# Expert results: from gated products on GpSimd, a scratch tensor and a closing pass, to products on VectorE and accumulating stores into the output rows

## The chip, the core and the metric

The kernel runs on one core of a Trainium2 chip. A core has TensorE (PE, matrix products into PSUM; PEld is its weight load), VectorE (DVE), ScalarE (ACT), GpSimd (POOL) and SyncE (SP, which here only issues transfers), each with an instruction queue of its own, and 16 DMA engines that move data between DRAM and SBUF. The engines wait for each other by semaphores. The metric is the device time of one launch in microseconds; the median of several runs is compared.

## The reference

A token mixer (two selective state-space scans, forward and backward) followed by a mixture of experts, for 2 batches of 2048 tokens of width 256. The part that the change touches is the end of it:

```
x = x + ga * mixer(...)
h = layernorm(x) * (1 + cb) + sb
# 8 experts, each token goes to its best 2, with weights from a softmax
for e in range(8):
    a  = silu(xs @ w1[e].T + b1[e])
    x2 = a @ w2[e].T + b2[e]
    x3 = xs @ w3[e].T + b3[e]
    y += sum over the token's two places of x2 * x3 * (expert of the place == e)
z = shared expert of h
x = x + gb * (y + z)        # gb: one row of 256 per batch
```

`xs` is the token's row times its routing weight. 4096 tokens with two experts each make 8192 (token, expert) pairs.

## The kernel before

The program is written by hand: each engine has a straight list of instructions, and the order of work is that list and the semaphore waits in it. There are three stages.

**Scan stage.** 16 steps of 16 units. It is not touched, but for a few constants that GpSimd makes in the last step (`constants`) for the stages behind.

**Router and shared expert.** A loop over 8 blocks of 512 tokens. SyncE loads a block (`load_block`), VectorE normalises and ranks the experts, TensorE and the others compute the shared expert, whose gated result VectorE adds to the block in `x1` (`add_shared`, semaphore `s_x1`). ScalarE scales the token's row by its weight into `send` (`scale_tokens`), adds the number of the pair as column 257, and GpSimd scatters the rows (`scatter`, an indirect transfer of 128 rows) to the region of the row's expert in `slot_scratch`. Places behind an expert's last row are filled with rows of zeros whose number points to spare rows ("trash"): ScalarE zeroes `send`, SyncE stores it twice (L676) early in the stage, ScalarE's first `scale_tokens` waits for both stores (`trash_kept`), and after all scatters SyncE copies one such row block behind each expert (L703).

**Expert stage.** 72 tiles of 128 rows (8192 pairs and up to one part-filled tile for each expert; spare tiles at the end). `tile_loop` writes out tiles 0 to 7, a hardware loop of 7 rounds of 8 tiles, and tiles 64 to 71. In tile s TensorE does the product with w1 and w3 of tile s (`hidden`, L1906), turns the silu of tile s-1 (L1916) and the input of tile s+1 (L1897), and does the product with w2 of tile s-2 (`result`, L1926). VectorE adds the biases: to the 512 columns of tile s (`bias_hidden`, L1555, into `hx`, ring of 4), copies the row numbers out (L1557, `target_u`), and to the 256 columns of tile s-2 (`bias_result`, L1564, into `yt`, ring of 4). Each of the two begins with a `value_load`: the engine's sequencer reads the tile's expert number from SBUF into a register and checks it, since the bias row is addressed by it. ScalarE copies and does silu. GpSimd multiplies x2 by x3 (L894) and stores the 128 rows by an indirect transfer (L898) to the row of their pair in `yout_scratch`. SyncE loads the input of tile s+4 (L696) when its buffer is free.

When all stores have landed comes a closing pass over 8 blocks: SyncE loads both results of each token from `yout_scratch` (L723), VectorE adds the two (L1583), multiplies by gb (L1585), adds to `x1` (L1587), and SyncE stores the block to the output (L692).

In the rows below the tiles' names are those of the tensor that the memory was first given to: `h` stands for the small tiles of the expert stage (xt, hx, hs, yt), `w` for the experts' weights and, in the closing pass, the loaded results.

## Time and profile before

| | |
|---|---|
| median of 3 runs | 2269.19 us (2267.29 to 2276.48) |
| the profiled execution | 2270.67 us |
| its span, first to last instruction | 2268.9 us |
| TensorE clock granted, mean | 0.853 |
| busy share | PE 80%, DVE 88%, ACT 61%, POOL 80% |

The span begins with the first instruction and ends with the last; the 1.8 us that the time has more lie around it. The shares are means over stages with different limits: DVE and POOL are busy nine tenths in the scan stage (up to about 1780 us), PE in the router stage and the expert stage (to about 2224 us), and neither in the closing pass.

### The profile page before, as it was taken

What the parts mean: (1) busy time and instruction counts of PE and PEld (TensorE: products, weight loads), DVE (VectorE), ACT (ScalarE), POOL (GpSimd) and SP (SyncE); (2) the same over time, 40 slices, a digit from 0 to 9 for tenths busy, and PEclk for the clock granted to TensorE, in tenths of its full rate; (3) what the DMA queues carried; (4) which work ended last, traced back from release to release, by engine and by line L of the source; (5) the groups of instructions that cost most, each with busy time, mean ns of one, the idle gap of its engine ahead of it and who ended that gap; (6) DMA issues with size and microseconds to landing.
All of it is one profiled execution on the core that took longest, in us unless ns stands there. A gap on an engine that the chain in (4) does not pass through costs nothing.

```text
span 2268.9 us, 23450 instructions
## 1 busy us (share of the span) xinstructions
PE 1821.4 (80%) x6088; PEld 754.4 (33%) x6089; DVE 2006.8 (88%) x2219; ACT 1374.9 (61%) x2348; POOL 1823.1 (80%) x718
## 2 busy tenths in 40 slices
PE   7687787978786978778797878797855799999991
PEld 3222232313231323223232323232321366656561
DVE  7899999999999999999999999999999876633335
ACT  4667768585867676776858576767755333323330
POOL 3499999999999999999999999999999443435551
PEclk9787888879787879788797979797967799999996
DMA  7734434343534344343434353444434541222226
GB/s 285 221 85 107 120 100 124 95 112 100 121 105 99 107 118 113 105 112 95 124 102 109 102 118 104 105 112 109 97 95 137 173 171 56 77 78 86 86 86 238
DMA packets 135965, 266.05 MB, mean 117 GB/s; under 512 B 20225, under 2 KB 39937, under 8 KB 134705
## 3 DMA queue, kind: packets, MB, share of 16 engines
q1 hardware_dynamic: 126448, 236.97, 38.9%
q0 software_dynamic: 6528, 17.87, 2.2%
q10 hardware_dynamic: 2880, 9.96, 1.1%
q8 instruction: 45, 0.74, 0.1%
q14 instruction: 64, 0.52, 0.1%
HBM read 198.62 MB, written 67.15 MB: 117 GB/s over the span
## 4 chain that ended last, share of the span: by engine, by line
DVE 43%; PE 25%; issue 14%; ACT 8%; POOL 6%; DMA 3%; SPq 1%; DVEq 0%; ACTq 0%; POOLq 0%
DVE hst L1315 28%; DVE dbu L1301 9%; PE psum L1906 6%; PE psum L1843 4%; POOL hst L800 4%; PE psum L1926 3%; ACT psum L1064 3%; PE psum L1718 2%; PE psum L1855 2%; PE psum L1652 2%; PE psum L1645 2%; PE psum L1676 1%; DMA b_rep<-bc_scratch 1%; ACT L1064 1%; PE psum L1706 1%
## 5 line engine op out<-in xcount | busy, mean ns | idle before, releaser
L800 POOL TENSOR_TENSOR hst<-hst,c_rep 128x2048 f32<-128x2048 f32 x255 | 1150.5, 4527 | 51.2 <-DVE hst L1315 31.8
L1064 ACT ACTIVATE psum<-dt_rep,neg_a 128x512 f32<-128x512 f32 x1024 | 687.9, 683 | 400.6 <-DVE hst L1315 398.7
L1315 DVE TENSOR_TENSOR_SCAN hst<-psum,state,dbu 128x512 f32<-128x512 f32 x768 | 920.8, 1254 | 0.0
L1301 DVE TENSOR_TENSOR dbu<-psum,b_rep 128x2048 f32<-128x2048 f32 x192 | 434.0, 2260 | 12.6 <-PE psum L1706 7.1
L1706 PE MATMUL psum<-dt,same 32*128 32x512 f32 x384 | 251.7, 739 | 171.7 <-DVE dbu L1301 166.9
L1718 PE MATMUL psum<-hst,same 128*32 128x512 f32 x2048 | 323.0, 788 | 79.3 <-POOL hst L800 71.0
L788 POOL TENSOR_TENSOR dbu<-dtu_rep,b_rep 128x2048 f32<-128x2048 f32 x64 | 291.4, 4553 | 25.8 <-DVE hst L1315 25.7
L1315 DVE TENSOR_TENSOR_SCAN hst<-psum,dbu 128x512 f32<-128x512 f32 x256 | 291.6, 1196 | 1.8 <-ACT psum L1064 1.7
L1664 PE MATMUL psum<-xp,taps 128*128 128x512 f32 x512 | 240.6, 614 | 2.1 <-DVE sp_tmp L1294 0.9
L1718 PEld LDWEIGHTS psum<-hst,same 128*32 128x32 f32 x2048 | 73.7, 139 | 340.5 <-issue 216.3
L1706 PEld LDWEIGHTS psum<-dt,same 32*128 32x128 f32 x384 | 64.4, 207 | 328.4 <-DVE dbu L1301 232.9
L1652 PE MATMUL psum<-xnT,w_in 128*128 128x512 f32 x256 | 139.8, 672 | 41.6 <-ACT sz L996 41.6
L1645 PE MATMUL psum<-xnT,w_in 128*128 128x512 f32 x256 | 132.8, 645 | 18.4 <-ACT xc L1008 17.4
L878 POOL DMA_INDIRECT slot_scratch<-send,slot_u x64 | 64.5, 1008 | 98.8 <-ACT send L1161 64.9
L1906 PE MATMUL psum<-w,h 128*128 x288 | 139.8, 608 | 1.9 <-ACT h L1182 1.9
L1664 PEld LDWEIGHTS psum<-xp,taps 128*128 128x128 f32 x512 | 96.7, 194 | 133.1 <-issue 130.8
L1555 DVE TENSOR_TENSOR h<-psum,b 128x512 f32<-128x512 f32 x72 | 49.8, 691 | 99.4 <-PE psum L1906 99.4
L1714 PE MATMUL psum<-xc,diag_d 128*128 128x512 f32 x128 | 97.3, 852 | 32.6 <-DVE sz L1286 32.5
L1676 PE MATMUL psum<-w_out,sz 128*128 128x256 f32 x512 | 119.2, 387 | 4.0 <-DVE sz L1286 4.0
L898 POOL DMA_INDIRECT yout_scratch<-h,target_u x72 | 72.5, 1008 | 59.4 <-POOL h L894 56.5
L1843 PE MATMUL psum<-h2T,sw 128*128 128x512 f32 x256 | 115.4, 605 | 1.4 <-ACT g_silu L1148 1.4
L1194 ACT ACTIVATE h<-psum 128x256 f32<-128x256 f32 x72 | 27.6, 383 | 143.7 <-PE psum L1916 143.7
(166 smaller groups left out, 2293.7 us busy)
## 6 DMA issues: line engine op xcount, KB each, us to landing
dt_rep<-dt_scratch SPq DMA_DIRECT2D x256, 256.0 KB, 4.5
taps<-taps_scratch SPq DMA_DIRECT2D x64, 256.0 KB, 3.0
b_rep<-bc_scratch SPq DMA_DIRECT2D x64, 256.0 KB, 5.1
c_rep<-bc_scratch SPq DMA_DIRECT2D x64, 256.0 KB, 7.9
dt_scratch<-dt SPq DMA_DIRECT2D x64, 256.0 KB, 2.0
dtu_rep<-dtu_scratch SPq DMA_DIRECT2D x256, 64.0 KB, 1.9
h<-slot_scratch SPq DMA_DIRECT2D x72, 128.5 KB, 2.1
sp_tmp<-t_scratch SPq DMA_DIRECT2D x16, 512.0 KB, 4.8
```

The costliest lines, as they stand in the source:

```text
L788: nc.gpsimd.tensor_tensor(dbu[:, U % DBU, :, :], dtu_rep[:].broadcast_to((P, NG, TB)), b_rep[U // UNITS % 2][:], ALU.mult).then_inc(pool_m ...
L800: nc.gpsimd.tensor_tensor(h, h, c_rep[q % 2][:], ALU.mult).then_inc(prod_done, 1)
L1064: nc.scalar.activation(psum[:, PS_A + i, :], dt_rep[:, G % 2, j, :], ACT.Exp, scale=neg_a[:, q % 2, u, i:i + 1]).then_inc(exp_done, 1)
L1301: nc.vector.tensor_tensor(dbu[:, U % DBU, :, :], psum[:, PS_U:PS_U + 1, :].broadcast_to((P, NG, TB)), b_rep[U // UNITS % 2][:], ALU.mult). ...
L1315: nc.vector.tensor_tensor_scan(time_order(hst[:, U % RING, i, :], backward), time_order(psum[:, PS_A + i, :], backward), time_order(dbu[:, ...
L1645: ins = nc.tensor.matmul(psum[:, bank, :], w_in[:, q % 2, k, c * P:(c + 1) * P], xnT[:, q % 2, k, :], start=(k == 0), stop=(k == KD - 1))
L1652: ins = nc.tensor.matmul(psum[:, bank, :], w_in[:, q % 2, k, DI + c * P:DI + (c + 1) * P], xnT[:, q % 2, k, :], start=(k == 0), stop=(k == ...
L1664: ins = nc.tensor.matmul(psum[:, bank, :], taps[:, c % 2, j, :], xp[:, c % 2, at:at + TB], start=(j == 0), stop=(j == TAPS - 1))
L1706: nc.tensor.matmul(psum[:, PS_U, :], same[part, :], dtu[part, c, :], start=True, stop=True).then_inc(u_full, 1)
L1718: ins = nc.tensor.matmul(psum[CH * j:CH * (j + 1), PS_Y, :], same[:, 0:CH], hst[:, (GN * G + j) % RING, i, :], start=False, stop=(i == NG ...
L1843: ins = nc.tensor.matmul(psum[:, bank, :], w[:, k, c * P:(c + 1) * P], h2T[:, j % 2, k, :], start=(k == 0), stop=(k == KD - 1))
L1906: ins = nc.tensor.matmul(psum[:, 2 + r % 2, :], xtT[:, r % 2, k * P:(k + 1) * P], w13[:, bass.ds(e * KD + k, 1), :].rearrange("p a n -> p ...
```

## The change

GpSimd no longer multiplies. VectorE does x2 times x3 (`bias_result`), and before it x3 times gb (`gate_rows`), for which it needs, row by row, gb of the row's batch: ScalarE makes half of it (`begin_gate`, gb of batch 0 times the row's first flag) and VectorE the rest; the two flags are two new columns of the scattered rows. The output tensor gets one row for each token; `x1` is stored to it block by block while the router loop runs (`store_block`), and GpSimd's indirect store of a tile adds its 128 rows to the output rows in DRAM (`compute_op=ALU.add`). Two experts can hold the same token, so a tile's store must not be in flight with one of the expert before: it waits for the stores of tiles s-2 and s-3 always, and for that of tile s-1 only where the expert changes; the count to wait for is looked up in a table (`follows_u`) by a `value_load`. The closing pass and `yout_scratch` are gone. The spare rows behind the output are set to zero by one more store.

```diff
 @@ router stage, SyncE
+            sp.dma_start(out[TOKENS:OUT_ROWS].rearrange("(a p) d -> p a d", p=P), trash[:, :, 0:DM]
+                         ).then_inc(trash_kept, 16)
...
+            def store_block(p):
+                n = TAKEN[p]
+                sp.wait_ge(s_x1, 2 * p + 2)
+                sp.dma_start(out[n * TB:(n + 1) * TB].rearrange("(p t) d -> p t d", t=NT), x1[:, rows_of(n), :]
+                             ).then_inc(f_out, 16)
             for p in range(4, NBLK):
                 load_block(p)
+                store_block(p - 4)
+            store_block(NBLK - 4)
...
 @@ expert stage, SyncE
             def tiles(s, r):
                 if not (isinstance(s, int) and s + 4 >= TILES):
                     sp.wait_ge(target_kept, s + 1)
+                    sp.wait_ge(gate_done, s + 1)
                     wait_apart(sp)
                     load_tile(s + 4, r)
...
-            for i in range(NBLK):
-                for k in range(2):
...
-                    sp.dma_start(yg[:, r, :].rearrange("p (t d) -> p t d", t=NT),
-                                 yout_dram[first:first + TB, :].rearrange("(t p) d -> p t d", p=P)
-                                 ).then_inc(y_back[r], 16)
-                if i >= 3:
-                    store_block(i - 3)
...
 @@ expert stage, GpSimd
             def tiles(s, r):
-                pool.wait_ge(y_biased, s + 1)
-                nc.gpsimd.tensor_tensor(yt[:, r % 4, :], yt[:, r % 4, :], hx[:, r % 4, DM:2 * DM], ALU.mult
-                                        ).then_inc(y_done, 1)
                 pool.wait_ge(y_done, s + 1)
+                for back in (3, 2):
+                    if not (isinstance(s, int) and s < back):
+                        pool.wait_ge(y_stored[(r - back) % 4], landed_by(s, r, back))
+                if isinstance(s, int) and s < 5:
+                    if s > 0:
+                        pool.wait_ge(y_stored[(r - 1) % 4], landed_by(s, r, 1))
+                else:
+                    count = nc.gpsimd.value_load(follows_u[0:1, bass.ds(s, 1)], min_val=16, max_val=4 * TILES)
+                    pool.wait_ge(y_stored[(r - 1) % 4], count)
                 wait_apart(pool)
                 nc.gpsimd.indirect_dma_start(
-                    yout_dram, bass.IndirectOffsetOnAxis(ap=target_u[:, r:r + 1], axis=0), yt[:, r % 4, :], None
-                    ).then_inc(y_stored[r % 4], 16)
+                    out, bass.IndirectOffsetOnAxis(ap=target_u[:, r:r + 1], axis=0), yt[:, r % 4, :], None,
+                    compute_op=ALU.add).then_inc(y_stored[r % 4], 16)
...
 @@ ScalarE
                 if m == 0:
-                    act.wait_ge(trash_kept, 32)
+                    act.wait_ge(trash_kept, 48)
...
+                nc.scalar.activation(send[:, m % 4, :, DM + 1:ROW],
+                                     batch_flag[:, n // SEG:n // SEG + 1, :].broadcast_to((P, NT, BATCH)), ACT.Copy
+                                     ).then_inc(scaled, 1)
...
+            def begin_gate(s, r, m):
+                act.wait_ge(xt_loaded[r % 4], m * 16 + 16)
+                if not (isinstance(s, int) and s < 2):
+                    act.wait_ge(gated, s - 1)
+                nc.scalar.activation(row_gate[:, r % 2, :], fmod[:, 0, 3, :], ACT.Copy, scale=xt[:, r % 4, DM + 1:DM + 2]
+                                     ).then_inc(gate_begun, 1)
...
 @@ expert stage, VectorE
+            def gate_rows(s, r):
+                dve.wait_ge(gate_begun, s + 1)
+                nc.vector.scalar_tensor_tensor(row_gate[:, r % 2, :], fmod[:, 1, 3, :], xt[:, r % 4, DM + 2:DM + 3],
+                                               row_gate[:, r % 2, :], ALU.mult, ALU.add).then_inc(gate_done, 1)
+                dve.wait_ge(gate_done, s + 1)
+                dve.wait_ge(hx_done, s + 1)
+                nc.vector.tensor_tensor(hx[:, r % 4, DM:2 * DM], hx[:, r % 4, DM:2 * DM], row_gate[:, r % 2, :], ALU.mult
+                                        ).then_inc(gated, 1)
...
                 nc.vector.tensor_tensor(yt[:, r % 4:r % 4 + 1, :], psum[:, 6 + r % 2:7 + r % 2, 0:DM],
                                         b2[:, bass.ds(e, 1), :], ALU.add).then_inc(y_biased, 1)
+                dve.wait_ge(y_biased, s + 1)
+                dve.wait_ge(gated, s + 1)
+                nc.vector.tensor_tensor(yt[:, r % 4, :], yt[:, r % 4, :], hx[:, r % 4, DM:2 * DM], ALU.mult
+                                        ).then_inc(y_done, 1)
 
             def tiles(s, r):
                 bias_hidden(s, r)
                 if not (isinstance(s, int) and s < 2):
                     bias_result(s - 2, (r - 2) % UNROLL)
+                gate_rows(s, r)
...
-            def finish(i):
...
-            for i in range(NBLK):
-                finish(i)
```

GpSimd's constants change by some small instructions, two small table instructions are added on VectorE behind the router loop, and the scattered rows are 259 numbers long, not 257.

On VectorE one tile of the hardware loop, the list before (ISA rows are register arithmetic of the sequencer; L1555 is `bias_hidden`, L1564 `bias_result`):

```order
L1551 TENSOR_LOAD expert_u
L1551 ISA x2
L1555 ISA [waits y_done,hx_full]
L1555 TENSOR_TENSOR h<-psum,b 128x512
L1557 CAST target_u<-h 128x1
L1560 TENSOR_LOAD expert_u
L1560 ISA x2
L1564 ISA [waits y_stored1,y_full]
L1564 TENSOR_TENSOR h<-psum,tin 128x256
```

And the same tile of the changed list (L1602 is `bias_hidden`, L1620 and L1624 are `bias_result`, L1608 and L1612 are `gate_rows`):

```order
L1602 TENSOR_TENSOR h<-psum,b 128x512
L1604 CAST target_u<-h 128x1
L1616 TENSOR_LOAD expert_u
L1616 ISA x2
L1620 ISA [waits y_stored1,y_full]
L1620 TENSOR_TENSOR h<-psum,tin 128x256
L1624 TENSOR_TENSOR h<-h 128x256 [waits gated,y_biased]
L1608 SCALAR_TENSOR_TENSOR h<-fmod,h 128x256 [waits gate_begun]
L1612 TENSOR_TENSOR h<-h 128x256 [waits hx_done,gate_done]
```

Three engine instructions came behind L1620, of which L1624 and L1612 wait for the instruction just before them; the TENSOR_LOAD of the next tile's `bias_hidden` now stands behind L1612, the last of them.

On GpSimd one tile of the hardware loop, before:

```order
L893 REGISTER_ALU
L894 TENSOR_TENSOR h<-h 128x256 [waits y_biased]
L898 DMA yout_scratch<-h,target_u 10240x256 [waits y_done]
L893 REGISTER_ALU
L894 TENSOR_TENSOR h<-h 128x256 [waits y_biased]
```

And in the changed list (L927 is the accumulating store, to the output):

```order
L916 REGISTER_ALU
L924 ISA [waits y_stored2,y_stored1,y_done]
L924 TENSOR_LOAD follows_u
L924 ISA x2
L927 DMA out_x<-h,target_u 6144x256 [waits y_stored3]
```

The product is gone from GpSimd; in its place stand a wait for two earlier stores, a register load, and a wait for the store just before.

## Rows read from the trace of the kernel before

**Rows 1.** Stretches: length, busy PE, PEld, DVE, ACT, POOL (count), clock, DMA share, GB/s
```profile
1950.00:2000.00 50.00, 46.51 (x163) 28.20 (x162) 21.49 (x56) 15.79 (x34) 15.71 (x16) 0.99 0.24 72
...
2170.40:2194.90 24.50, 24.50 (x97) 14.62 (x96) 9.41 (x24) 8.30 (x24) 13.77 (x17) 1.00 0.28 86
...
2220.60:2268.90 48.30, 2.59 (x11) 1.56 (x10) 30.04 (x27) 0.59 (x2) 5.56 (x7) 0.58 0.78 271
```

**Rows 2.** TensorE's branch at the end of the hardware loop's rounds
```profile
L491 PEldq COMPARE_BRANCH  x7: 83/227/247, 2047.8 to 2194.9; - x7
```

**Rows 3.** Timeline: the last hidden tile
```profile
2219.67 0.69 DVE L1555 TENSOR_TENSOR h<-psum,b 128x512 f32<-128x512 f32 x1 [1.32 <-PE psum L1906]
```

**Rows 4.** The chain that ended last, closing pass: start, us, what
```profile
2264.64 1.22 DVE x L1587
```

**Rows 5.** Groups by line in the expert stage
```profile
L898 POOL DMA_INDIRECT yout_scratch<-h,target_u x72 | 72.5, 1008 | 59.4 <-POOL h L894 56.5 <-issue 3.0
L894 POOL TENSOR_TENSOR h<-h 128x256 f32<-128x256 f32 x72 | 51.5, 715 | 64.8 <-DVE h L1564 64.6
```

**Rows 6.** Timeline, one tile of the hardware loop
```profile
2103.57 0.69 DVE L1555 TENSOR_TENSOR h<-psum,b 128x512 f32<-128x512 f32 x1 [1.22 <-PE psum L1906]
...
2104.87 0.42 DVE L1564 TENSOR_TENSOR h<-psum,tin 128x256 f32<-128x256 f32 x1 [0.55 <-PE psum L1926]
```

**Rows 7.** VectorE's sequencer (DVEq), 2103.5 to 2106.7: min/median/max ns, first and last start
```profile
L1563 DVEq EVENT_SEMAPHORE  x1: 21/21/21, 2104.3 to 2104.3; - x1
L1551 DVEq TENSOR_LOAD <-expert_u x1: 303/303/303, 2105.0 to 2105.0; - x1
L1554 DVEq EVENT_SEMAPHORE  x1: 21/21/21, 2105.7 to 2105.7; - x1
L1555 DVEq FUSED_REGOPS  x2: 57/57/57, 2103.5 to 2106.5; - x2
```

**Rows 8.** Timeline: three kinds of VectorE instruction on 256 columns
```profile
1797.08 1.66 DVE L1345 SCALAR_TENSOR_TENSOR h<-x,fmv,fmod 128x256 f32<-128x256 f32 x4
...
1801.35 0.43 DVE L1384 TENSOR_TENSOR cmp_eq<-score 128x256 f32<-128x256 f32 x1
1801.81 0.42 DVE L1385 TENSOR_TENSOR cmp_eq<-cmp_eq,lower 128x256 f32<-128x256 f32 x1
```

**Rows 9.** One line's own durations (ns)
```profile
L1345 DVE SCALAR_TENSOR_TENSOR h<-x,fmv,fmod x32: 474/478/480, 1786.8 to 1943.5; 128x256 f32<-128x256 f32 x32
```

**Rows 10.** VectorE and GpSimd at the same time (timeline)
```profile
1777.62 3.27 DVE L1482 TENSOR_TENSOR hst<-hst,c_rep 128x2048 f32<-128x2048 f32 x1
...
1769.77 8.97 POOL L800 TENSOR_TENSOR hst<-hst,c_rep 128x2048 f32<-128x2048 f32 x2
...
1816.86 0.43 DVE L1384 TENSOR_TENSOR cmp_eq<-score 128x256 f32<-128x256 f32 x1
...
1816.46 1.27 POOL L878 DMA_INDIRECT slot_scratch<-send,slot_u  x1 [0.20 <-issue]
```

**Rows 11.** Transfers of the expert stage: KB each, median us to landing
```profile
h<-slot_scratch SPq DMA_DIRECT2D x72, 128.5 KB, 2.1
...
yout_scratch<-h,target_u POOLq DMA_INDIRECT x72, 2.5
slot_scratch<-trash_scratch SPq DMA_DIRECT2D x3, 128.5 KB, 2.6
```

**Rows 12.** SyncE: eight transfers, each behind a value_load
```profile
1983.20 9.53 SPq L703 DMA_DIRECT2D slot_scratch<-trash_scratch  x8
```

**Rows 13.** Early router stage: transfers, and the timeline behind the trash stores
```profile
slot_scratch<-send SPq DMA_DIRECT2D x1, 1028.0 KB, 13.7
...
1784.63 0.58 SPq L676 DMA_DIRECT2D slot_scratch<-send  x1
...
1806.26 1.69 ACT L1159 ACTIVATE send<-h,weight 128x256 f32<-128x256 f32 x4
...
1810.02 1.22 PE L1843 MATMUL psum<-h2T,sw 128*128 128x512 f32 x1 [1.41 <-ACT g_silu L1148]
```

More of the change, by code:

```diff
@@ L429, in mixer_and_experts @@
         target_kept = sem("target_kept")
-        y_back = [sem(f"y_back{r}") for r in range(8)]
-        f_fin = sem("f_fin")
+        gate_begun = sem("gate_begun")
+        gate_done = sem("gate_done")
+        gated = sem("gated")
         f_out = sem("f_out")
@@ L2002 @@
            for name, v in arrays.items()}
[L2003 removed]
+    out = nc.dram_tensor("out_x", (OUT_ROWS, DM), F32, kind="ExternalOutput").ap()
     mixer_and_experts(nc, aps, out)
```

81 lines of the change are left out of this document (44 added, 37 removed).

## Prediction, made before the change was run

> **What bounds the kernel now.** I read the profile from its end. The stretch behind the last tiles ([rows 1], third row) is 48.3 us long and holds 2.6 us of TensorE work: this is the closing pass. The timeline of the last tiles and the chain of waits give its place: VectorE adds the bias to the last hidden tile at 2219.67 [rows 3], its last instruction of the closing pass starts at 2264.64 [rows 4], and the span ends at 2268.9. From that bias addition, which I call H, to the end are 49.2 us.
>
> Before it, in the expert stage, TensorE is busy all of the time at full clock, 24.50 of 24.50 us in one round of 8 tiles, VectorE 9.4 us [rows 1], its second row. The branch at a round's end comes seven times from 2047.8 to 2194.9 [rows 2], so a tile takes 147.1 / 48 = 3.065 us. TensorE sets this pace, and whatever the change puts on other engines is free only while their own time for a tile stays below 3.065 us.
>
> The shares hide one thing: VectorE's 9.4 us of 24.5 counts instructions, not its sequencer. Between an instruction and one behind a `value_load`, the sequencer reads and checks the register. After the bias addition at 2104.87 [rows 6] it reaches the wait behind the load only at 2105.7, and the next instruction's own register step and start take 0.1 more (2106.5 to 2106.6) [rows 7]: 0.8 + 0.06 + 0.1, about 0.95 to 1.0 us. The other load begins at 2103.57 [rows 6] and its wait is reached at 2104.3 [rows 7]; with the register step the earliest start of L1564 is 0.95 us behind that of L1555. Today both stand in time that VectorE would idle anyway.
>
> **The closing pass goes.** What takes its place is the way of the last results to DRAM. After H VectorE adds the bias of tile 69 (0.9 us on), multiplies (0.46 more to its start, 0.42 long): the product of 69 is ready at H + 1.8. Behind that come the gate of tile 71 (to its last issue 2.2 us on) and the last two bias additions, each behind a load of 0.8 us and each followed by its product: bias of 70 at H + 3.0, its product 0.5 on, bias of 71 at H + 4.3 to 4.4, its product ready at H + 5.3. For one store GpSimd then needs a register load (not in this trace on GpSimd; on SyncE eight transfers with one each take 9.53 us in all [rows 12], so a pitch of 1.29 with some 0.5 of transfer instruction, which leaves 0.8), the 0.8 us that the indirect store now starts behind its releaser (59.4 / 72 [rows 5]), and the landing, 2.5 us behind the start for the plain store [rows 11].
>
> The trace has no accumulating store. From below: a copy DRAM to DRAM of 128 rows lands in 2.6 us and a read of as many in 2.1 us [rows 11], so an added read can be nearly free: 2.5 us. From above: a read and a write in series, 2.1 + 2.5 = 4.6 us, unless the adding itself is slow, which no row excludes. I take 3.5 us, the middle. One store is then 0.8 + 0.8 + 3.5 = 5.1 us from its releaser to its landing. Tile 69 lands at H + 6.9, tile 71 waits for it and lands at H + 12.0, and the end comes some 0.4 us later. Saved: 49.2 - 12.4 = **36.8 us**.
>
> **What GpSimd's waits cost in the loop.** The chain through GpSimd is "the store two tiles back has landed, then 5.1 us": 2.55 us for a tile, less than TensorE's 3.065. At an expert's first tile it is 5.1 us for one tile, some 2 us late, eight times at most. Queued behind is the next store alone, and who waits for stores is VectorE's `bias_result` of four tiles on, 12 us later. So I cost these waits at nothing; the cover is the ring of four, and it goes if the landing takes more than about 5 us (below).
>
> **VectorE gets the products.** Per tile: a scalar_tensor_tensor (0.478 us [rows 9]) and two tensor_tensor of 256 columns (0.42 us each [rows 8]). By busy time VectorE has 9.41 / 8 = 1.18 us a tile and would have 2.50: fits under 3.065. By its list it does not. From the start of L1602: 0.95 to the bias addition L1620; 0.46 to the product L1624, since an instruction that waits for its predecessor starts 0.46 behind it (1801.35 to 1801.81 [rows 8]), and 0.03 for its second wait; 0.34 to L1608, which waits for nothing late (independent ones overlap by 0.085: four of 0.478 in 1.66 us [rows 8, 9]); 0.48 + 0.04 to L1612, which waits for L1608, and 0.03 for its second wait; then the load of the next tile, 0.95 to 1.0, which now begins only when L1612 has been issued. Sum: 0.95 + 0.49 + 0.34 + 0.55 + 1.0 = **3.33 us**. VectorE's sequencer becomes the bound of the loop, though VectorE's busy share stays at three quarters.
>
> In the tiles written out the loads need no address arithmetic and the sum is about 3.10. Against before: 56 tiles x (3.33 - 3.065) = 14.8, seven branches of VectorE's own at 0.15 = 1.0, 15 tiles x 0.06 = 0.9: **+16.7 us**. The five terms are each good to some 0.03 to 0.05 us, so the tile may come to 3.2 as well as to 3.45.
>
> [...] VectorE's record here is 0.303 us [rows 7]. [...]
>
> **ScalarE** gets one instruction of 256 columns, and has 8.30 of 24.5 us busy [rows 1]: free, and its result is asked for one tile later. **SyncE's** loads wait for L1608 of tile s, some 2 us later than now, with three tiles (9 us) in hand and 2.1 us to landing: free. PE's clock: a stretch with TensorE 93% busy had 0.99 ([rows 1], its first row), and at 3.33 us a tile it is 92% busy, so I leave it at full.
>
> **The router stage.** Eight stores of 512 KB of `x1` lie in a stage in which the DMA engines are a quarter busy; SyncE's waits for `s_x1` come before those for the later loads anyway: nothing. The zeroing of the spare rows is another matter. Both trash stores (2.1 MB) are issued by 1784.63 and the second lands 13.7 us later, at 1798.3 [rows 13]. 2.1 MB more behind them at the same 230 to 280 GB/s lands at 1805.8 to 1807.4. ScalarE's first scaling, at 1806.26, waits for it, and TensorE stands 1.41 us for ScalarE at 1810.02 [rows 13]: so this instruction is on the path. I take +0.6 us, and +0.2 for the flag column's instruction, here and before the last scatter. GpSimd's constants are some short instructions in gaps of the scan stage: nothing.
>
> **Sum**, against the profiled execution: 2270.67 - 36.8 + 16.7 + 0.8 = 2251.4 us. The profiled execution lies 1.5 us over the median, so **2250 us** is what I forecast for the median.
>
> **The rivals.**
> *VectorE keeps up* (chance 0.16). If the sequencer runs further ahead than I read, the loop stays at 3.065: 2250 - 16.7 = 2233 us. For it: the busy time of 2.50 us. Against: in rows 6 and 7 the load always starts behind the instruction before it.
> *The accumulating store is slow* (0.13), the one that ends on the other side. Two landings back means (1.6 + L) / 2 us a tile, with L from start to landing; at L = 5.1 that is my 3.33. The gain is gone at L = 5.4: 71 x ((1.6 + 5.4) / 2 - 3.06) + 2 x 1.9 = 35 us. At L = 6 it is 3.8 us a tile, 2233 + 52.5 + 5 = 2291 us. For it: no row shows the adding. Against: the 4.6 us of a read and a write in series.
> *GpSimd and VectorE hold each other up* (0.04). VectorE's product of 2048 columns with two SBUF inputs took 3.27 us, to 1780.89, beside GpSimd's products, which ended at 1778.74; the 2.15 us from there are just what 2048 columns take at 0.42 us for 256 with the start taken off, so it had waited [rows 10]. If GpSimd's indirect store held VectorE so, each tile would wait 0.3 to 1.0 us, and the time would be about 2250 + 72 x 0.5 = 2286 us. Against: beside L878 the product L1384 took its 0.43 us, and it was GpSimd that took 1.27 [rows 10]. [...]
>
> **How the numbers follow.** The likeliest, VectorE's list as the bound, has 0.64, with a range of its own of 2243 to 2259; the last 0.03 are for what I don't see. 0.5% of 2269 is 11.3 us, about what a measurement of this kernel can tell from no change. Faster by more (under 2257.8): the first rival's 0.16, some 0.53 of the likeliest, 0.01 of the slow store: 0.70. Within: the likeliest's upper tail, a tile of 3.45 us or a landing of 5 us: 0.18. Slower (over 2280.5): most of the slow store and of the contention: 0.12. The range of 2232 to 2268 leaves out the slow cases and takes in the first rival.
>
> **What the profile will show.** In a round of the hardware loop of 26 to 27.5 us instead of 24.5: TensorE under 95% busy, with waits for ScalarE's silu and, through it, for VectorE's L1602; L1602 no longer waiting for L1906. Starts of L1612 and the next L1602 0.95 to 1.0 us apart. The accumulating store landing 3 to 4 us behind its start, GpSimd idle for stores only at experts' first tiles. The end 12 us behind the last L1602. The first L1188 at 1806.5 to 1808. Wrong it goes first if the landing is over 5 us, if TensorE's clock falls at 92% busy, or if rounds are 24.5 us as before.

## The result, and the profile after

| | before | after |
|---|---|---|
| median of 5 runs, us | 2269.86 (2267.29 to 2276.48) | 2255.35 (2247.88 to 2256.75) |
| profiled execution, us (its span) | 2270.67 (2268.9) | 2256.75 (2255.0) |

The ratio on record is 0.9924, 95% interval 0.9911 to 0.9938: faster by 0.76%. (It is not the ratio of the two medians, which differ by 14.5 us, 0.64%.) 19 us were forecast.

The stretches that answer to [rows 1]: the router's last part, one round of 8 tiles and somewhat less, and the last tiles with the end.
```profile
1950.00:2000.00 50.00, 47.51 (x173) 29.54 (x171) 23.00 (x60) 15.80 (x37) 15.94 (x16) 1.00 0.26 87
2180.00:2204.60 24.60, 24.12 (x88) 13.33 (x88) 17.89 (x47) 11.13 (x30) 11.61 (x8) 1.00 0.50 80
2220.60:2255.00 34.40, 23.43 (x90) 13.50 (x89) 20.32 (x50) 10.19 (x28) 15.74 (x11) 0.94 0.45 62
```
The end with almost no TensorE work is gone, and VectorE does twice the work in a stretch of the loop (17.89 us in 24.6, where it was 9.41 in 24.5). TensorE reads as busy at 98%, and yet it completes 88 matmuls in 24.6 us where it completed 97 in 24.5: the ends of matmuls are modelled, so its busy time hides that it is being kept waiting. The granted clock stayed at 1.00 in the loop. What tells the pace is the branch at a round's end, which answers to [rows 2]:
```profile
L499 PEldq COMPARE_BRANCH  x7: 83/227/246, 2053.5 to 2215.4; - x7
```
161.9 us for 48 tiles are 3.373 us a tile (3.065 before). The groups by line of the expert stage say who waits. VectorE's hidden bias before:
```profile
L1555 DVE TENSOR_TENSOR h<-psum,b 128x512 f32<-128x512 f32 x72 | 49.8, 691 | 99.4 <-PE psum L1906 99.4
```
and the lines of after:
```profile
L927 POOL DMA_INDIRECT out_x<-h,target_u x72 | 113.0, 1569 | 155.2 <-DMA out_x<-h,target_u 70.3 <-issue 47.0 <-DVE h L1624 37.9
L1602 DVE TENSOR_TENSOR h<-psum,b 128x512 f32<-128x512 f32 x72 | 49.8, 692 | 53.1 <-issue 39.7 <-PE psum L1950 13.4
L1620 DVE TENSOR_TENSOR h<-psum,tin 128x256 f32<-128x256 f32 x72 | 30.6, 425 | 14.7 <-issue 8.8 <-PE psum L1970 1.3 <-DMA out_x<-h,target_u 0.6
```
VectorE's hidden bias waited for TensorE before (99.4 us in all); now 39.7 of its 53.1 us are "issue", time in which nothing that the profile shows was awaited. VectorE's result bias waits 0.6 us in all for landed stores. Of the 70.3 us that the profile puts to landings ahead of GpSimd's stores, 31 are no wait. The profile names the semaphore that came last, and at this pace a store often lands just when the next one starts (a landing takes 3.7 us or more, and from the store at 2172.74 to the next at 2176.45 are 3.71). In the trace GpSimd lags its data by up to 8.6 us at the first tiles and has caught up by tile 24; from there to tile 67 a store starts 1.4 to 1.8 us behind the end of its product whether or not a landing is named, and 2.2 to 3.1 us behind it at five tiles, where it waits for the store before. One tile of VectorE's timeline, to be laid beside [rows 6]:
```profile
2101.49 0.69 DVE L1602 TENSOR_TENSOR h<-psum,b 128x512 f32<-128x512 f32 x1 [0.59 <-issue]
2102.10 0.14 DVE L1604 CAST target_u<-h 128x1 uint32<-128x1 f32 x1
2102.36 0.42 DVE L1620 TENSOR_TENSOR h<-psum,tin 128x256 f32<-128x256 f32 x1
2102.81 0.42 DVE L1624 TENSOR_TENSOR h<-h 128x256 f32<-128x256 f32 x1
2103.16 0.48 DVE L1608 SCALAR_TENSOR_TENSOR h<-fmod,h 128x256 f32<-128x256 f32 x1
2103.67 0.42 DVE L1612 TENSOR_TENSOR h<-h 128x256 f32<-128x256 f32 x1
2104.93 0.69 DVE L1602 TENSOR_TENSOR h<-psum,b 128x512 f32<-128x512 f32 x1 [0.84 <-issue]
```
From L1602 to L1620, L1624, L1608, L1612 and the next L1602 the starts are 0.87, 0.45, 0.35, 0.51 and 1.26 us apart (the last one 0.98 at the tile behind it). The sequencer's rows for its two register reads show why the last one varies (ns, shortest/median/longest):
```profile
L1598 DVEq TENSOR_LOAD <-expert_u x72: 300/311/632, 1999.2 to 2240.6; - x72
...
L1616 DVEq TENSOR_LOAD <-expert_u x72: 297/303/676, 2011.5 to 2245.4; - x72
```
Most reads take 0.30 us; 15 of the 144 take over 0.45, the longest 0.68. `expert_u` is the table of the tiles' expert numbers, which the kernel keeps in SBUF. The other two parts of this `value_load` are register arithmetic, 0.19 us in the median, and the check of the value, 0.02 us:
```profile
L1598 DVEq FUSED_REGOPS  x121: 53/190/211, 1999.8 to 2241.1; - x121
...
L1598 DVEq SEQ_ASSERT  x72: 23/23/35, 2000.0 to 2241.3; - x72
```

The end, on the timeline, answers to [rows 3, 4]: the last hidden bias, which the prediction calls H, and the last four stores (tiles 68 to 71).
```profile
2241.53 0.69 DVE L1602 TENSOR_TENSOR h<-psum,b 128x512 f32<-128x512 f32 x1 [0.48 <-issue]
...
2242.88 1.55 POOL L927 DMA_INDIRECT out_x<-h,target_u  x1 [2.94 <-DMA out_x<-h,target_u]
...
2245.03 1.55 POOL L927 DMA_INDIRECT out_x<-h,target_u  x1 [0.60 <-issue]
...
2248.08 1.55 POOL L927 DMA_INDIRECT out_x<-h,target_u  x1 [1.49 <-DVE h L1624]
2250.02 1.57 POOL L927 DMA_INDIRECT out_x<-h,target_u  x1 [0.39 <-issue]
```
From H to the end are 13.5 us (49.2 before). The chain of waits has the stores' way to DRAM (start, us):
```profile
2238.38 3.70 DMA out_x<-h,target_u
2242.88 3.76 DMA out_x<-h,target_u
```
To cut the execution into stages, I take the first and the last start of the hidden bias, of before and after:
```profile
L1555 DVE TENSOR_TENSOR h<-psum,b x72: 690/691/693, 2002.5 to 2219.7; 128x512 f32<-128x512 f32 x72
```
```profile
L1602 DVE TENSOR_TENSOR h<-psum,b x72: 691/692/693, 2005.6 to 2241.5; 128x512 f32<-128x512 f32 x72
```
and the last links of the scan in the chain of waits, of before and after:
```profile
1770.45 7.08 DVE hst L1315 x6
```
```profile
1772.60 7.08 DVE hst L1358 x6
```

| stage | before | after | difference | forecast |
|---|---|---|---|---|
| to the scan's last links | 1770.5 | 1772.6 | +2.1 | 0 |
| router, to the first hidden bias | 232.1 | 233.0 | +0.9 | +0.8 |
| first to last hidden bias | 217.1 | 235.9 | +18.8 | +16.7 |
| H to the end | 49.2 | 13.5 | -35.7 | -36.8 |

The sum, -13.9, is the difference of the two profiled executions. Of the signs that the prediction named, most came: 27.0 us for a round of 8 tiles, landings of 3.7 to 4.4 us in the chain of waits, 13.5 us behind the last L1602. TensorE under 95% busy did not: it reads as 98%.

### The profile page after: what moved, and what is told of

The parts are those of the page before. It is cut to its first block, busy times and chain, and to the rows that moved or that the text cites. A ratio compares the mean times of both kernels' runs of the same rounds, so it can differ in the third digit from the quotient of the medians.

```text
span 2255.0 us, 24227 instructions
## 1 busy us (share of the span) xinstructions
PE 1829.4 (81%) x6088; PEld 756.1 (34%) x6089; DVE 2068.6 (92%) x2413; ACT 1409.9 (63%) x2436; POOL 1811.8 (80%) x652
## 3 DMA queue, kind: packets, MB, share of 16 engines
q0 software_dynamic: 13440, 17.93, 4.8%
## 4 chain that ended last, share of the span: by engine, by line
DVE 49%; PE 16%; issue 16%; ACT 10%; DMA 4%; DVEq 3%; POOL 2%; SPq 1%; POOLq 0%; ACTq 0%
DVE hst L1358 31%; DVE dbu L1344 10%; PE psum L1887 4%; ACT psum L1093 3%; PE psum L1696 3%; PE psum L1899 2%; PE psum L1762 2%; DMA out_x<-h,target_u 2%; ACT L1093 1%; PE psum L1750 1%; POOL hst L807 1%; DVEq L1598 1%; DVE h L1608 1%; DVE sz L1329 1%; DVE h L1620 1%
## 5 line engine op out<-in xcount | busy, mean ns | idle before, releaser
L1344 DVE TENSOR_TENSOR dbu<-psum,b_rep 128x2048 f32<-128x2048 f32 x192 | 436.3, 2273 | 15.7 <-PE psum L1750 9.9
L1750 PE MATMUL psum<-dt,same 32*128 32x512 f32 x384 | 257.5, 755 | 158.1 <-DVE dbu L1344 153.3
L1762 PE MATMUL psum<-hst,same 128*32 128x512 f32 x2048 | 306.1, 752 | 86.6 <-POOL hst L807 78.0
L927 POOL DMA_INDIRECT out_x<-h,target_u x72 | 113.0, 1569 | 155.2 <-DMA out_x<-h,target_u 70.3
L1696 PE MATMUL psum<-xnT,w_in 128*128 128x512 f32 x256 | 150.4, 718 | 48.4 <-ACT sz L1025 48.4
L1689 PE MATMUL psum<-xnT,w_in 128*128 128x512 f32 x256 | 132.1, 642 | 18.4 <-ACT xc L1037 17.4
L1738 PE MATMUL psum<-sp_tmp,w_dt 16*128 16x512 f32 x128 | 94.1, 843 | 43.1 <-ACT sp_tmp L1064 42.4
L1720 PEld LDWEIGHTS psum<-w_out,sz 128*128 128x128 f32 x512 | 97.0, 192 | 35.7 <-issue 18.1
L1758 PE MATMUL psum<-xc,diag_d 128*128 128x512 f32 x128 | 88.2, 777 | 21.1 <-DVE sz L1329 20.3
```

The source lines that it names most:

```text
L1344: nc.vector.tensor_tensor(dbu[:, U % DBU, :, :], psum[:, PS_U:PS_U + 1, :].broadcast_to((P, NG, TB)), b_rep[U // UNITS % 2][:], ALU.mult). ...
L1696: ins = nc.tensor.matmul(psum[:, bank, :], w_in[:, q % 2, k, DI + c * P:DI + (c + 1) * P], xnT[:, q % 2, k, :], start=(k == 0), stop=(k == ...
L1720: ins = nc.tensor.matmul(psum[:, bank, half * DM:(half + 1) * DM], sz[:, c, tok], w_out[:, q % 2, c, :], start=(c == 0), stop=(c == NC - 1))
L1750: nc.tensor.matmul(psum[:, PS_U, :], same[part, :], dtu[part, c, :], start=True, stop=True).then_inc(u_full, 1)
L1762: ins = nc.tensor.matmul(psum[CH * j:CH * (j + 1), PS_Y, :], same[:, 0:CH], hst[:, (GN * G + j) % RING, i, :], start=False, stop=(i == NG ...
```

## The experiments

The theory: VectorE's sequencer sets the pace of the loop, by register reads in series with waits. The rivals: GpSimd's accumulating store sets it, or VectorE's executing time, or the three products contend with the stores. Each kernel below is the changed kernel with the edit shown, or with several where it says so. "A tile" is the branch's first to last time over 48.

**One read more.**
```diff
             def bias_result(s, r):
+                nc.vector.value_load(expert_u[0:1, bass.ds(s, 1)], min_val=0, max_val=NE - 1)
                 e = nc.vector.value_load(expert_u[0:1, bass.ds(s, 1)], min_val=0, max_val=NE - 1)
```


> VectorE reads the expert number once more for each tile, right ahead of the read for the result's bias; nothing else changes. If VectorE's sequencer sets the pace of the loop (my theory), each tile gets longer by what the added read takes there: 0.30 us for the record of the load, about 0.2 us of register arithmetic and 0.02 us of range check, 0.5 to 0.55 us in all, so a tile goes from 3.37 to some 3.9 us and the time from 2255 to 2255 + 72 x 0.53 = 2293 us. If VectorE's executing time or TensorE sets the pace (the rival that VectorE keeps up, or a loop that is slower for GpSimd's store), an added read is hidden and the time stays at 2255.


Measured: 2294.1 us (ratio to before 1.0108, 1.0080 to 1.0136), 3.960 us a tile:
```profile
L499 PEldq COMPARE_BRANCH  x7: 83/227/251, 2056.6 to 2246.7; - x7
```
0.59 us more for each tile (0.5 to 0.55 expected), none of it hidden. VectorE's busy time for a tile did not rise; its list did.

**The number kept in a register.**
```diff
             def bias_hidden(s, r):
                 e = nc.vector.value_load(expert_u[0:1, bass.ds(s, 1)], min_val=0, max_val=NE - 1)
+                numbers[r] = e
...
-            def bias_result(s, r):
-                e = nc.vector.value_load(expert_u[0:1, bass.ds(s, 1)], min_val=0, max_val=NE - 1)
+            def bias_result(s, r, kept=True):
+                e = numbers[r] if kept else nc.vector.value_load(expert_u[0:1, bass.ds(s, 1)], min_val=0, max_val=NE - 1)
...
-                    bias_result(s - 2, (r - 2) % UNROLL)
+                    bias_result(s - 2, (r - 2) % UNROLL, r > 1)
```


> VectorE keeps the expert number read for the hidden bias in a register and uses it again for the result's bias two tiles later, so 54 of the 72 second reads go (in each run of 8 tiles the first two results still read theirs). If the sequencer sets the pace, the bias addition L1620 starts 0.70 to 0.75 us behind L1602 and not 0.87 to 0.95, since L1602 itself takes 0.69: 0.15 to 0.2 us less in 6 of 8 tiles, a tile of 3.23 to 3.26 us and 2255 - 9 = 2246 us (2243 to 2249). If something else sets the pace (GpSimd's store or TensorE), no change: 2255.


Measured: 2246.3 us (0.9898, 0.9879 to 0.9918), 3.258 us a tile, as expected. (56 of the 72 second reads are gone, not 54.)

**Another order, both reads kept.**
```diff
                 bias_hidden(s, r)
+                fill_gate(s, r)
                 if not (isinstance(s, int) and s < 2):
                     bias_result(s - 2, (r - 2) % UNROLL)
                 gate_rows(s, r)
+                if not (isinstance(s, int) and s < 2):
+                    gate_result(s - 2, (r - 2) % UNROLL)
```
`fill_gate` has the scalar_tensor_tensor L1608 that stood in `gate_rows`, and `gate_result` the product L1624 that stood in `bias_result`, each with its waits.


> The same instructions of VectorE in another order, both reads kept: hidden bias, gate of the rows (scalar_tensor_tensor), result's bias, product with the gate, product of the result. No instruction waits any more for the one right ahead of it. By my list: 0.71 to the gate, 0.90 behind the read to the result's bias, 0.40 and 0.40 to the two products, 0.95 behind the next read: 3.36 us a tile against 3.37, so no change, 2252 to 2256 us, since the reads still follow each other with 0.8 us of sequencer each. If what costs is the waits for VectorE's own results (0.49 and 0.55 in my sum, the rival reading), the two shorter pitches give 0.2 us a tile and the time is 2241.


Measured: 2244.7 us (0.9881, 0.9860 to 0.9902), and the tile fell to 3.075 us: TensorE's pace. My list was wrong. The rival reading was right in kind, and gave 0.2 us a tile where 0.30 went; the median stayed above its 2241. The timeline, and the sequencer's read of the result's number (L1618) in the same tile:
```profile
2103.53 0.69 DVE L1602 TENSOR_TENSOR h<-psum,b 128x512 f32<-128x512 f32 x1 [0.65 <-PE psum L1958]
2104.14 0.14 DVE L1604 CAST target_u<-h 128x1 uint32<-128x1 f32 x1
2104.20 0.47 DVE L1608 SCALAR_TENSOR_TENSOR h<-fmod,h 128x256 f32<-128x256 f32 x1
2104.94 0.42 DVE L1622 TENSOR_TENSOR h<-psum,tin 128x256 f32<-128x256 f32 x1 [0.26 <-PE psum L1978]
2105.28 0.41 DVE L1614 TENSOR_TENSOR h<-h 128x256 f32<-128x256 f32 x1
2105.61 0.42 DVE L1628 TENSOR_TENSOR h<-h 128x256 f32<-128x256 f32 x1
```
```profile
L1618 DVEq TENSOR_LOAD <-expert_u x1: 600/600/600, 2103.6 to 2103.6; - x1
```
The read starts at 2103.6, ahead of the cast (2104.14) and of the gate (2104.20), which stand before it in the program. So the sequencer hands instructions on and reads ahead, while they wait their turn. Even a read of 0.60 us is hidden. In the changed kernel each of L1624 and L1612 waits for the instruction right ahead of it, and that wait holds the sequencer: the next read starts only behind the start of L1612.
```profile
L1598 DVEq TENSOR_LOAD <-expert_u x1: 582/582/582, 2103.8 to 2103.8; - x1
```
That is the read at the tile above: L1612 started at 2103.67, the read at 2103.8 (0.10 us behind it in the median of all tiles). Other work lies between producer and consumer in the new order: L1614 and L1628 start 0.34 and 0.33 us behind the instruction ahead, where L1624 and L1612 of the changed kernel start 0.45 and 0.51 us behind the one they wait for.

**No read at all.** The order and the waits of the changed kernel; the biases are those of expert 0 for every tile, so the other experts' biases are left out.
```diff
-                e = nc.vector.value_load(expert_u[0:1, bass.ds(s, 1)], min_val=0, max_val=NE - 1)
+                e = 0
```


> VectorE reads no expert number: both bias additions take the rows of expert 0 for every tile (a change of the computation: biases of the other experts are left out), so both register reads, their checks and the address arithmetic go, and the order and all waits of the changed kernel stay. If the two reads are what makes the list long, the sum is 0.71 + 0.49 + 0.34 + 0.55 + 0.62 = 2.7 us a tile, TensorE sets the pace again at 3.07 and the time is 2236 to 2241. If waits for VectorE's own results or the store are enough by themselves, the tile stays at 3.3 and the time at 2252 or more.


Measured: 2240.7 us (0.9873, 0.9855 to 0.9892), 3.067 us a tile. So neither the reads nor the waits make the loop slow by themselves: it takes both, in series. The accumulating store and all three products are still there, so neither the store nor VectorE's executing time is the bound.

**Both edits.** The kept number and the other order.


> The kept number and the other order together. By the list of VectorE's sequencer: 0.71 + 0.40 + 0.40 + 0.40 + 0.95 = 2.86 us where the number is kept, which is under TensorE's 3.065, and about 3.3 in the two tiles of 8 with a second read: a mean of 3.10 to 3.13, so 2255 - 72 x 0.25 = 2237 us (2233 to 2242). If GpSimd's accumulating store is what makes the loop slower than before, there is no gain here: 2255.


Measured: 2236.6 us (0.9852, 0.9832 to 0.9873), 3.067 us a tile:
```profile
L499 PEldq COMPARE_BRANCH  x7: 83/227/246, 2044.4 to 2191.6; - x7
```
The time is the expected one, the tile is shorter than the 3.10 to 3.13 of my list. In the loop the other order alone does as much. The two profiled executions are 15.7 us apart all the same: 13.2 of it lie ahead of the tiles, and behind the last hidden bias the other order took 17.3 us and this kernel 14.5, since GpSimd's stores ran later there. How much of the 8 us between the medians is the edit's is not shown. What remained in the trace was one late stretch near the start, where VectorE's bias waits for a place in the ring of four:
```profile
2040.46 0.42 DVE L1625 TENSOR_TENSOR h<-psum,tin 128x256 f32<-128x256 f32 x1 [2.81 <-DMA out_x<-h,target_u]
```
It comes from GpSimd's first stores, which the program always lets wait for the one before (at tiles 1 to 4 the table's count is 0 where the expert does not change, and the kernel's register load is set to take 16 or more):
```profile
2015.12 1.55 POOL L927 DMA_INDIRECT out_x<-h,target_u  x1 [3.10 <-DMA out_x<-h,target_u]
2020.13 1.55 POOL L927 DMA_INDIRECT out_x<-h,target_u  x1 [3.46 <-DVE h L1631]
2024.81 1.65 POOL L927 DMA_INDIRECT out_x<-h,target_u  x1 [3.13 <-DMA out_x<-h,target_u]
```

**A free start**, on top of both edits.
```diff
+            for r in range(4):
+                nc.gpsimd.dma_start(dtu_dram[0, r:r + 1], dtu_dram[1, r:r + 1]).then_inc(y_stored[r], 16)
+            for r in range(4):
+                pool.wait_ge(y_stored[r], 16)
...
-                if isinstance(s, int) and s < 5:
-                    if s > 0:
-                        pool.wait_ge(y_stored[(r - 1) % 4], landed_by(s, r, 1))
-                else:
+                if not (isinstance(s, int) and s == 0):
```
(and every count on `y_stored` 16 higher).


> The kept number and the other order, and besides that the first stores no longer always wait for the one before: the four landing semaphores begin at 16 (a tiny copy for each, waited for ahead of the tiles), so that the register's value can be used from the second tile on. In the run with both edits the first five stores start 4.7 us apart, GpSimd is 6 us behind its tiles by then, and VectorE's bias additions at tiles 11 to 15 come 3 us late in sum because the ring of four is full. If that reading is right, those 3 us go: 2236.5 - 3 = 2233.5 us (2231 to 2235). If the late tiles have another cause, 2236.5.


Measured: 2236.3 us (0.9840, 0.9815 to 0.9865). The hidden biases of both edits and of this kernel:
```profile
L1605 DVE TENSOR_TENSOR h<-psum,b x72: 690/692/693, 1996.6 to 2216.4; 128x512 f32<-128x512 f32 x72
```
```profile
L1606 DVE TENSOR_TENSOR h<-psum,b x72: 690/692/693, 2003.0 to 2220.3; 128x512 f32<-128x512 f32 x72
```
From first to last: 219.8 and 217.3 us, so the late stretch is gone from the trace (before had 217.1). But the profiled execution reached its tiles 6.4 us later; the scan's last links started 6.5 us later, in a stage that both have alike. The two were timed once more, side by side:


> The kernel with both edits once more, timed beside the next two: 2236 us, between 2233 and 2239.

> The kernel with the free start once more, beside the one above. The late tiles 11 to 15 went in the trace of its first run (217.3 us from the first to the last hidden bias against 219.8), so it should be 2.5 us faster than the one above: ratio 0.9989. If front stages differ by more than that between runs, the difference is not told apart.


Measured: 2236.4 us (0.9853, 0.9835 to 0.9871) and 2241.2 us (0.9859, 0.9836 to 0.9883), with 219.2 and 217.4 us between the hidden biases. The 2 us are real in the trace and not to be told in the time, since runs of the second spread over 14 us (2230.8 to 2245.1).

**No wait at the spare tiles**, on top of the free start.
```diff
+            counted(nc.vector.tensor_scalar(expert[:], expert[:], float(NE - 1), None, ALU.min))
+            settle()
             counted(nc.vector.tensor_tensor(changes[:, 1:TILES], expert[:, 1:TILES], expert[:, 0:TILES - 1],
                                             ALU.not_equal))
```


> The free start, and the mark of an expert's first tile is worked out after the numbers are cut to the last expert, so the first spare tile no longer waits for the last real tile. In the trace of the free start that store starts 4.44 us behind the one before it, at 2222.41, and could start at 2220.8; with the two-back waits behind it the last landing comes 1.5 to 1.8 us earlier. One more short instruction of VectorE ahead of the tiles costs 0.2. So 1.5 us faster than the free start, 2232 to 2234 us; if the last stores are set by their data and not by this wait, no difference.


Measured: 2237.4 us (0.9853, 0.9831 to 0.9875). In its trace the last hidden bias is at 2222.0 and the span ends at 2235.6: 13.6 us, where the free start had 14.3 in both its traces (2220.3 to 2234.6 in the first). 0.7 us and not 1.5 to 1.8, and not to be told in the time.

**The product back on GpSimd**, ahead of its store, everything else as changed.
```diff
             def tiles(s, r):
+                pool.wait_ge(y_biased, s + 1)
+                pool.wait_ge(gated, s + 1)
+                nc.gpsimd.tensor_tensor(yt[:, r % 4, :], yt[:, r % 4, :], hx[:, r % 4, DM:2 * DM], ALU.mult
+                                        ).then_inc(y_done, 1)
                 pool.wait_ge(y_done, s + 1)
...
-                dve.wait_ge(y_biased, s + 1)
-                dve.wait_ge(gated, s + 1)
-                nc.vector.tensor_tensor(yt[:, r % 4, :], yt[:, r % 4, :], hx[:, r % 4, DM:2 * DM], ALU.mult
-                                        ).then_inc(y_done, 1)
```


> The product of the result with the gated x3 goes back to GpSimd, ahead of its accumulating store; the rest is as in the changed kernel. VectorE's list then is 0.9 + 0.34 + 0.55 + 1.0 = 2.8 us a tile, under TensorE's 3.065. GpSimd's own list is 0.72 for the product, some 0.9 for the wait for it, the register load and the check, 1.57 for the store's descriptors and 0.1 to 0.3 to the next start: 3.3 to 3.5 us a tile. My theory: GpSimd takes VectorE's place as the bound, 3.4 us a tile, 2250 to 2262 us, no gain from undoing this part. The rival: VectorE's list was the only thing too long and GpSimd has room, 3.07 us a tile and 2235.


Measured: 2308.9 us (1.0180, 1.0152 to 1.0208), slower than before, 193.7 / 48 = 4.035 us a tile. GpSimd is the bound, as I said, but by far more than the 3.4 us that I said. The gate's product on VectorE, the product on GpSimd, GpSimd's store, and one store with the product behind it:
```profile
L1616 DVE TENSOR_TENSOR h<-h x72: 424/832/1387, 2002.8 to 2285.0; 128x256 f32<-128x256 f32 x72
```
```profile
L918 POOL TENSOR_TENSOR h<-h x72: 741/1315/1567, 2009.6 to 2297.5; 128x256 f32<-128x256 f32 x72
```
```profile
L931 POOL DMA_INDIRECT out_x<-h,target_u x72 | 115.4, 1603 | 121.0 <-DMA out_x<-h,target_u 95.3 <-DVE h L1616 17.0 <-issue 8.8
```
```profile
2123.36 1.73 POOL L931 DMA_INDIRECT out_x<-h,target_u  x1 [1.63 <-DMA out_x<-h,target_u]
2124.54 1.32 POOL L918 TENSOR_TENSOR h<-h 128x256 f32<-128x256 f32 x1
```
GpSimd's product takes 1.3 and not 0.715 us [rows 5], but VectorE is not the cause: the product in the last line runs from 2124.54 to 2125.86, and VectorE has no instruction between 2124.09 and 2126.00. The product's record begins some 0.55 us before that of the store ahead of it ends, and ends some 0.76 us behind it (0.75 to 0.77 at nearly all tiles), so it stands in line behind GpSimd's own store; at three tiles only, beside a VectorE product of 1.36 to 1.39 us, it took 1.57. From store to store are then 1.60 for the store, 0.76 for the product and 121.0 / 72 = 1.68 us before the next store, 4.04 in all. I had 1.57, 0.72 and 1.0 to 1.2: the term that I had too small is the time between the product and the store, with the wait for the product and the register load in it. VectorE's product is held up: it took 0.83 us or more at the 46 tiles where GpSimd's product ran beside it, and its 0.42 us at the other 26. Since VectorE waited for GpSimd in this kernel (98.3 of the 106.8 us that it stood idle ahead of the hidden biases are put to L918), this is not what set its pace. In the changed kernel, where GpSimd has the indirect store alone, VectorE's two-input products keep their 0.425 us:
```profile
L1624 DVE TENSOR_TENSOR h<-h x72: 424/425/491, 2013.2 to 2246.7; 128x256 f32<-128x256 f32 x72
...
L1612 DVE TENSOR_TENSOR h<-h x72: 424/424/429, 2006.8 to 2244.1; 128x256 f32<-128x256 f32 x72
```

**A plain store.** The results overwrite the output rows and are not added to them, so the output is not the sum.
```diff
-                    out, bass.IndirectOffsetOnAxis(ap=target_u[:, r:r + 1], axis=0), yt[:, r % 4, :], None,
-                    compute_op=ALU.add).then_inc(y_stored[r % 4], 16)
+                    out, bass.IndirectOffsetOnAxis(ap=target_u[:, r:r + 1], axis=0), yt[:, r % 4, :], None
+                    ).then_inc(y_stored[r % 4], 16)
```


> The indirect stores of the tiles overwrite the output rows and do not add to them (the output is then not the sum): all waits, loads and orders stay. By the trace of before the descriptors take 1.01 us of GpSimd and not 1.57, and a store lands some 2.5 us behind its start and not 3.7. If VectorE's list sets the pace of the loop, only the end gains: the last stores by 3 to 4 us, so 2251 to 2253 us, and the landing in the loop changes nothing. If the accumulating store is what makes a tile 3.37 us (the rival that it is slow), the loop falls to 3.07 a tile and the time to 2232.


Measured: 2252.3 us (0.9909, 0.9881 to 0.9938), 158.4 / 48 = 3.300 us a tile.
```profile
L927 POOL DMA_INDIRECT out_x<-h,target_u x72 | 69.2, 961 | 193.4 <-DMA out_x<-h,target_u 115.9 <-issue 41.3 <-DVE h L1623 36.2
```
```profile
out_x<-h,target_u POOLq DMA_INDIRECT x72, 2.4
```
Adding costs 1.569 against 0.961 us of GpSimd and 3.7 to 4.4 against 2.4 us to landing. (The store is one record on GpSimd; that this time goes to its descriptors, as the expectations have it, was my reading and is not shown.) The loop stays slow without it, so the store is not its bound; but 0.07 us a tile, 3.5 us over the hardware loop, did go, which I had at nothing. The register reads give them back. The read ahead of the hidden bias, in the hardware loop of this kernel and of the changed one:
```profile
L1597 DVEq TENSOR_LOAD <-expert_u x48: 300/305/315, 2063.7 to 2218.5; - x48
```
```profile
L1598 DVEq TENSOR_LOAD <-expert_u x49: 301/310/632, 2053.4 to 2215.2; - x49
```
The 96 reads of the hardware loop add up to 29.2 us here, none over 0.32, and to 32.5 us in the changed kernel, ten over 0.45. That is 3.3 of the 3.5 us. The slow reads do not come at random: 14 of the 15 in the changed kernel's trace end 2.4 to 2.8 us behind the start of an accumulating store, and 8 of the 9 in the kernel before end 1.9 to 2.0 us behind the start of a plain one. So they seem to meet something that a store does, in either kind; what, is not shown, and with plain stores this kernel's reads just miss it. Behind the last hidden bias this kernel took 11.0 us, 2.5 less than the changed one (3 to 4 expected). Its median cannot be told from that of the changed kernel.

**A wait at every tile** for the store before.
```diff
-                for back in (3, 2):
+                for back in (3, 2, 1):
...
-                if isinstance(s, int) and s < 5:
-                    if s > 0:
-                        pool.wait_ge(y_stored[(r - 1) % 4], landed_by(s, r, 1))
-                else:
-                    count = nc.gpsimd.value_load(follows_u[0:1, bass.ds(s, 1)], min_val=16, max_val=4 * TILES)
-                    pool.wait_ge(y_stored[(r - 1) % 4], count)
```


> Each store waits until the one before it has landed, at every tile and not only where the expert changes; the register read of GpSimd goes. In the changed kernel the stores that wait in this way start 4.5 to 4.9 us behind each other, so GpSimd sets the pace at 4.6 us a tile: 2014.5 + 71 x 4.6 + 4 = 2345 us for the last landing, 2335 to 2360 in all. By the 5.1 us from releaser to landing of the prediction it would be 2380. If waits for landed stores were covered by the ring of four, it would stay at 2255.


Measured: 2373.1 us (1.0461, 1.0432 to 1.0490), 240.9 / 48 = 5.02 us a tile: more than the 4.6 from the stores that wait once in a while, and close to the 5.1 us of the prediction's chain. The mark of an expert's first tile, which lets all other stores go without this wait, is worth 118 us.

## Why the prediction was right, and where its sizes were off

The forecast of 2250 us lies 5.4 us under the median, and the measured time is inside its range. The steps did not cancel: the profiled execution is 5.4 us over its sum of 2251.4, 1.1 from the end, 2.1 from the loop, 0.1 from the router and 2.1 from the scan, all the same way. By its steps:

- **The closing pass.** Right: -35.7 against -36.8 us. The accumulating store's landing was put at 3.5 us, in the middle of 2.5 and 4.6, a choice between two bounds and not a reading, so some luck is in it; it took 3.7 at the end. Tile 71's store starts at H + 8.5, and SyncE, which waits for the last landing, goes on at 2253.9, which is H + 12.3, against 12.0. Most of the 1.1 us is what comes behind the last landing: 1.1 to 1.2 us and not 0.4.
- **GpSimd's waits cost nothing in the loop.** Right in this kernel: they reach VectorE with 0.6 us, and once GpSimd has caught up, by tile 24, it waits for landings in the loop at five tiles alone, as forecast for experts' first tiles. Not seen was that the first stores wait at every tile, four times and not only where the expert changes. The slow loop covered that; in the kernel with both edits it costs 2.5 us.
- **VectorE's sequencer becomes the bound.** Right, shown from three sides: a read more costs 0.59 us a tile, no read brings back 3.067, another order brings back 3.075. The term was mis-sized: the tile took 3.373 and not 3.33, since reads were priced at the one row of 0.303 us while some take 0.6 (what they take over 0.303 adds up to 3.5 us in the hardware loop, 0.07 a tile, so the other pitches were 0.03 too long), and the 15 written-out tiles cost some 1.6 us and not 0.9 (the first seven pitches end at 21.6 instead of 21.2 us, the last eight at 25.5 instead of 24.3). Together +18.8 and not +16.7.
- **"The load always starts behind the instruction before it"**, the sentence against the first rival. This was wrong as a rule, though it gave nearly the right number. The trace of before has a read ahead of an instruction not yet started, in the same tile: the cast stands before it in the program and starts 0.5 us behind it.
```profile
L1560 DVEq TENSOR_LOAD <-expert_u x1: 303/303/303, 2103.7 to 2103.7; - x1
```
```profile
2104.17 0.14 DVE L1557 CAST target_u<-h 128x1 uint32<-128x1 f32 x1
```
In these traces the sequencer reads ahead of instructions not yet started, unless it stands at a wait that is not met: in the changed list, one for VectorE's own result, with the next read 0.10 us behind the start of L1612. My expectation for the other order used the same rule and missed by 0.29 us a tile.
- **The router.** +0.9 against +0.8, but the reason given for most of it did not hold. The zeroing of the spare output rows was issued at 1787.43 and took 17.3 us to land, to 1804.7; ScalarE's first scaling, at 1808.63, came later than that and waited for TensorE's part of the chain. The flags cost 0.09 us behind the instruction before them. And the stage itself varies by more than the difference: in the other twelve traces, of kernels that share it with the changed one, it took 231.7 to 233.9 us, where before had 232.1. So the match of 0.9 with 0.8 is luck, and the traces do not tell whether the stage got longer.
- **The scan.** +2.1 us of the profiled execution was not forecast and is not put down to the change: the same link of the chain starts at 1764.07 in the kernel with the kept number and in the one with both edits, at 1775.88 in the one with the other order, with the same instructions up to there.

Of the rivals, "VectorE keeps up" fell for this order of instructions and holds for another. The slow store fell: 3.7 to 4.4 us to landing, under the 5.4 at which it decides. GpSimd does hold VectorE up when both multiply (0.83 us or more for a product of 0.42), but the changed kernel has no product on GpSimd any more. The product on VectorE is a part of what makes its list too long, and still it saves 53 us by the medians against leaving it on GpSimd ahead of the accumulating store.

The best kernels are those with both edits: 2236 us, 1.5% under before and 0.8% under the changed one. The two further edits can't be told from it in the time.

## What to carry to other kernels

Count an engine's list and not its busy share: VectorE was 73% busy (17.89 of 24.6 us) and yet the bound. A register read ahead of an instruction was free here (3.075 us a tile with both reads, TensorE's pace) as long as no unmet wait, above all one for the engine's own last result, stood ahead of it; so put an independent instruction between a producer and its consumer, and keep a number in its register instead of reading it again. Before a product moves to GpSimd, add up GpSimd's list too: here the store, the product behind it and the time to the next store made 4.0 us a tile. A difference of 1 us in a stage says little before it is known how far the stage varies between kernels that do not differ in it: here by 2.2 us.

## What the runs showed of the hardware

- VectorE's sequencer ran at least two instructions ahead in the other order: a read began 0.5 us before the cast that stands ahead of it had started, and before the gate behind the cast. In the changed kernel a wait on a result of its own stopped this: the next read's register step came 0.01 us behind the start of L1612, the read 0.10.
- A register read took 0.30 to 0.31 us in the median and up to 0.71 us (L1618 in the other order), its register arithmetic 0.19 and its check 0.02 us. The slow ones in the changed kernel, over 0.45 us, end 2.4 to 2.8 us behind the start of an accumulating store, 14 of 15. One read more, with its arithmetic and check, cost 0.59 us a tile where nothing covered it (3.960 against 3.373).
```profile
L1618 DVEq TENSOR_LOAD <-expert_u x72: 299/312/707, 2015.9 to 2233.1; - x72
```
- GpSimd's product that follows its indirect store is on record with 1.31 us instead of 0.715, since its record begins some 0.55 us before the store's has ended; 0.76 us of it lie behind that end.
- With accumulating indirect stores of 128 rows of 1 KB the queue had 13440 packets, with plain ones 6528, for the same 17.9 MB; the software queue of the changed kernel and of the plain store:
```profile
q0 software_dynamic: 13440, 17.93, 4.8%
```
```profile
q0 software_dynamic: 6528, 17.93, 2.2%
```
- The stages ahead of the router, the same in all kernels, ended up to 13 us apart between profiled executions (the scan's last links from 1764.1 in the kept number to 1777.2 in the plain store). A change of 2 us can be read between the first and the last hidden bias (219.8 and 219.2 us for both edits, 217.3 and 217.4 with the free start) and not in the time of the whole.
